# A recurrent attention layer and a split-precision FFN on one core: x loaded in both layouts, shifts on GpSimd, branch bodies exchanged, a new order on every engine

## The chip, the cores and the metric

One core of a Trainium2 chip. The metric is device time of one execution in microseconds. PE is TensorE, DVE is VectorE, ACT is ScalarE, POOL is GpSimd, SP is the engine that issues DMAs here.

## What is computed

x has 8 sequences of 1024 tokens of 128 values. The layer is a gated linear attention with 16 heads of 8 values, then a layer norm, then a gated FFN with ternary weights times scales (here multiplied by 8), then a layer norm:

```python
def step(state, inp):
    qt, kt, vt, gt = inp
    state = state * gt[..., None] + vt[..., None] * kt[..., None, :]
    out_t = jnp.einsum('bhij,bhj->bhi', state, qt)
    return (state, out_t)
...
out = (out - mu) * jax.lax.rsqrt(var + EPS) * gamma + beta
out = out * jax.nn.silu(x @ Wg)
return out @ Wout
...
h = jax.nn.silu(_tlin(x, w1_w, w1_s)) * _tlin(x, w2_w, w2_s)
h = jax.nn.gelu(_tlin(h, h1_w, h1_s), approximate=False)
h = jax.nn.gelu(_tlin(h, h2_w, h2_s), approximate=False)
return _tlin(h, w3_w, w3_s)
...
x = _layernorm(x + attention(x))
x = _layernorm(x + ffn(x))
```

Here q, k, v are x times Wq, Wk, Wv, the gate g is sigmoid(x @ Wf + bf), and the FFN is 128 to 512, 512 to 512 twice, 512 to 128.

## The kernel before

The tokens are cut into 16 blocks of 512 (two to a sequence), and block n passes through five parts on five engines. All engines run hand-ordered lists: a loop over steps s, and in each step calls for block s, s-1, s-2 and so on, so that parts of several blocks lie side by side. There is no scheduler at run time; an instruction waits on semaphores named at its start, and everything behind it on its engine waits too. The text says "step" for one turn of this loop, and the step's length is the time per block.

**Front.** transpose_x (L633) turns the four 128x128 pieces of x_in into `front`, one PSUM bank; ACT copies it to xT. From xT come k, q, the forget gate f and the output gate, one product each into the same bank `front`, each waiting until ACT has emptied it (`freed`), and v into `ps_v`. k and q go out to a buffer in HBM (`send`) and come back (`fetch`) spread over 128 partitions as KJ and QJ, 8 slices of 512, in halves of 1 MB.

**Attention on DVE.** kv (L439) multiplies v by K, two slices at a time, scan (L449) runs the recurrence for one slice, qs (L460) multiplies by Q, two slices at a time, and add (L466) folds the halves. sum_transposed on PE adds the rest while transposing, into `back`. This bank also serves norm_o, the transposed o, the product with Wout, the transposed x1, and the FFN's last product.

**Norms.** There are three per block, "o", "1" and "2". DVE takes statistics (L470) and aggregates them to mean and variance (L474) in `mv`; POOL adds eps and raises to -0.5 (rstd_of, L223 and L225); DVE multiplies -mean by rstd (shift_of, L491); ACT applies both to four chunks (L302). rstd and shift have one buffer each, so rstd_of of the next block waits for norm_done.

```python
e.tensor_tensor(rstd[k][:], mv[k][:, :, 1], eps4[:], ALU.add).then_inc(ve_done[k], 1)
e.wait_ge(ve_done[k], n + 1)
e.tensor_tensor(rstd[k][:], rstd[k][:], mhalf4[:], ALU.pow).then_inc(rstd_done[k], 1)
```

**FFN.** Values are split into a high part (ACT, a copy rounded to fp32r: x1hi, h1hi, h2hi) and a low part (POOL subtracts, L216, 512 columns each; x1lo on DVE). PE multiplies both by the weights: up_hi, up_lo (L695, L706), mid_open, mid_hi, mid_lo for two layers (L711, L737), last_begin and last_rest (L741). Silu and gelu are on ACT (L331, L344), hmul on DVE (L511), which multiplies the two halves of the gated layer.

**Low parts of the weights.** At the start the weights are split too (split_weights on ACT, wlo on POOL); their low parts are summed, counted, and the count set as a flag. PE reads the flag (value_load, then a branch) once, before step 3. If there are low parts, a body with extra products runs; if not, as here, the Else body:

```python
with e.If(n_low != 0):
    for s in range(FIRST_UP, NB + 4):
        step(s, True)
with e.Else():
    for s in range(FIRST_UP, NB + 4):
        step(s, False)
```

Of the kernel before, what the change touches and what calls it, by code (L numbers as in the profile page):

```python
# [3 lines left out]
def build_program(nc, x_d, wproj_d, wffn_d, w3_d, w3s_d, cols_d, ident_d, out_d):  # L4
# [8 lines left out]
    B, S, D = x_d.shape  # L13
# [11 lines left out]
    assert D == P and PER_SEQ == 2 and NB % 2 == 0 and NH == 4  # L25
# [6 lines left out]
    with ctx:  # L32
# [3 lines left out]
        def sem(name):  # L36
# [16 lines left out]
        mhalf4 = sb("mhalf4", [P, NC_])  # L53
        low_sum = sb("low_sum", [P, 4])
# [5 lines left out]
        xT = sb("xT", [P, T])  # L60
# [18 lines left out]
            for name, shape in (("stats", (NC_, 6)), ("mv", (NC_, 2)), ("rstd", (NC_,)), ("shift", (NC_,))))  # L79
# [13 lines left out]
        def landed(n):  # L93
# [3 lines left out]
        q_sent, k_sent, stored = ([sem(f"{k}{p}") for p in range(2)] for k in ("q_sent", "k_sent", "stored"))  # L97
        K_landed, Q_landed = (
            [[sem(f"{k}{half}_{p}") for p in range(2)] for half in range(2)] for k in ("K_landed", "Q_landed"))
        xT_made, q_made, k_made, v_made, f_made, gate_made = (  # L100
            sem(f"{k}_made") for k in ("xT", "q", "k", "v", "f", "gate"))
# [4 lines left out]
        xT_copied, q_copied, k_copied = (sem(f"{k}_copied") for k in ("xT", "q", "k"))  # L106
# [9 lines left out]
        stats_done, mv_done, ve_done, rstd_done, shift_done, norm_done = (  # L116
            {k: sem(f"{name}_{k}_done") for k in "o12"} for name in ("stats", "mv", "ve", "rstd", "shift", "norm"))
# [25 lines left out]
        def _(e):  # L143
# [30 lines left out]
            e.dma_start(ident[:], ident_d).then_inc(consts_landed, 16)  # L174
            load_x(0)
            e.dma_start(wproj[:].rearrange("p c d -> p (c d)"), wproj_d).then_inc(consts_landed, 16)
            e.dma_start(cols[:], cols_d).then_inc(consts_landed, 16)
            load_x(1)
# [5 lines left out]
            for s in range(NB + 6):  # L184
                n = s - 2
                if live(n):
                    fetch(n, 1, 0)
                    send(n, 0)
                    fetch(n, 1, 1)
                    fetch(n, 0, 0)  # L190
# [3 lines left out]
                n = s - 2  # L194
                if live(n):
                    fetch(n, 0, 1)
# [4 lines left out]
                if live(n):  # L201
                    if n > 1:
                        load_x(n)
# [7 lines left out]
        def _(e):  # L211
# [15 lines left out]
            e.wait_ge(consts_set, 5)  # L227
            for s in range(NB + 3):
                if s == 0:
                    for k, (raw, cs) in enumerate(staged):  # L230
                        e.wait_ge(whi_done, k + 1)
                        for a in range(cs.start, cs.stop, T):
                            e.tensor_tensor(wlo[:, a:a + T], raw[:, a - cs.start:a - cs.start + T], whi[:, a:a + T].bitcast(f32),
                                            ALU.subtract).then_inc(wlo_done, 1)
                    e.wait_ge(w3_landed, 32)
                    e.tensor_tensor(w3[:], w3[:], w3_scale[:].unsqueeze(1).broadcast_to([P, NH, D]), ALU.mult).then_inc(w3_scaled, 1)
                n = s - 2
                if live(n):
                    lo(2, n, 0)
                n = s - 1  # L240
                if live(n):
                    rstd_of(n, "1")
                n = s - 2
                if live(n):
                    lo(2, n, 1)
                    lo(2, n, 2)
                    lo(2, n, 3)
                n = s - 3
# [3 lines left out]
                if live(n):  # L252
                    lo(1, n, 0)
                    lo(1, n, 1)
                n = s
                if live(n):
                    rstd_of(n, "o")
                n = s - 1
                if live(n):
                    lo(1, n, 2)  # L260
                    lo(1, n, 3)

        @block.scalar
        def _(e):
            def copy_xT(n):
                e.wait_ge(xT_made, n + 1)
                if n:
                    e.wait_ge(gate_made, n)
                e.activation(xT[:], front[:], ACT.Copy).then_inc(xT_copied, 1)

# [28 lines left out]
            def normalise(n, k, dst, src):  # L299
                e.wait_ge(shift_done[k], n + 1)  # L300
                for c in range(NC_):
                    last = e.activation(dst[:, chunk(c)], src[:, chunk(c)], ACT.Identity,  # L302
                                        bias=shift[k][:, c:c + 1], scale=rstd[k][:, c:c + 1])
# [56 lines left out]
            e.wait_ge(consts_set, 5)  # L360
            for s in range(NB + 5):
                n = s - 4
                if live(n):
                    hi(1, n, 2)
                n = s - 1
                if live(n):
                    copy_k(n)
                n = s - 4
                if live(n):
                    hi(1, n, 3)  # L370
                n = s - 3
                if live(n):
                    norm_o(n)
                n = s - 1
                if live(n):
                    copy_q(n)
                    if n == 0:
                        split_weights()
                n = s - 3
                if live(n):  # L380
                    affine(n)
                n = s - 4
                if live(n):
                    gelu(1, n, 0)
                    hi(2, n, 0)
                    gelu(1, n, 1)
                    gelu(1, n, 2)
                    hi(2, n, 1)
                    gelu(1, n, 3)
                    hi(2, n, 2)  # L390
                    hi(2, n, 3)
                n = s - 3
                if live(n):
                    norm_1(n)
                    x1_hi(n)
                n = s - 4
                if live(n):
                    gelu(2, n, 0)
                n = s - 1
                if live(n):  # L400
                    tanh(n)
                    if n == 1:
                        sum_low_parts()
                n = s - 4
                if live(n):
                    gelu(2, n, 1)
                    gelu(2, n, 2)
                    gelu(2, n, 3)
                n = s - 3
                if live(n):  # L410
                    silu(n, 0)
                    silu(n, 1)
                n = s - 1
                if live(n):
                    silu_gate(n)
                    g_of_tanh(n)
# [4 lines left out]
                if live(n):  # L421
                    hi(1, n, 0)
# [4 lines left out]
                if live(n):  # L427
                    copy_xT(n)
# [482 lines left out]
```

## Time and profile before

| | us |
|---|---|
| median of 3 runs | 584.1 (582.96 to 585.02) |
| the profiled execution | 584.93 |
| its span, first to last instruction | 582.5 |
| busy: PE, DVE | 520.5, 497.1 |
| busy: ACT, POOL | 395.1, 241.1 |
| mean granted TensorE clock | 0.955 |

A page of the profile lists for each engine how long it was busy; the 40 slices show that DVE and PE are over nine tenths busy from about the fifth slice to the 35th, and that the ends are looser. The rows below are from several views: groups by line, the timeline in order of time, waits (who waited for whom), the chain of work that ended last, and busy time in windows. Ends of PE's products are modelled, so in a busy stretch the distance between starts is the better measure.

### The profile page before, as it was taken

The page shows a single profiled execution, that of the slowest core. Times are in us where ns is not written, and L with a number is a line of the kernel's source. Part 1 is how long each engine was busy: PE and PEld are TensorE (multiplying, and loading weights), DVE is VectorE, ACT ScalarE, POOL GpSimd, SP SyncE. Part 2 cuts the span into 40 slices and gives each one's busy share as a digit, 9 for nine tenths or more (in the row PEclk, how much of TensorE's full clock was granted, in tenths as well). Part 3 has the DMA queues.
Part 4 walks back from the last instruction along what each step waited for, and adds up shares of the span by engine and source line. Part 5 has one row for each costly group of instructions (what it writes and reads, how often), then busy time and mean ns, then how long its engine had stood idle before and what let it go on. Part 6 is the DMA issues. An engine that isn't in the chain of part 4 may idle for free.

```text
span 582.5 us, 7709 instructions
## 1 busy us (share of the span) xinstructions
PE 520.5 (89%) x2536; PEld 391.6 (67%) x2536; DVE 497.1 (85%) x871; ACT 395.1 (68%) x685; POOL 241.1 (41%) x239
## 2 busy tenths in 40 slices
PE   4546289999999999999999999999999999888994
PEld 1114157868787777778786878777777778666863
DVE  0397599999999999999999999999999999894311
ACT  2552157777777777777787777777777778676753
POOL 0900045152534445453616253544545362535460
PEclk9667689999999999999999999999999999899998
DMA  7899909476684929392948668593929297000001
GB/s 287 204 247 238 230 5 236 107 181 162 154 208 115 248 71 251 78 257 68 254 109 204 157 166 196 137 224 86 257 73 266 58 252 170 0 20 0 19 0 37
DMA packets 32056, 87.82 MB, mean 151 GB/s; under 512 B 2320, under 2 KB 18960, under 8 KB 23568
## 3 DMA queue, kind: packets, MB, share of 16 engines
q1 hardware_dynamic: 32016, 87.31, 60.7%
q8 instruction: 22, 0.36, 0.3%
q14 instruction: 18, 0.15, 0.1%
HBM read 74.72 MB, written 12.58 MB: 150 GB/s over the span
## 4 chain that ended last, share of the span: by engine, by line
DVE 59%; PE 19%; issue 8%; ACT 5%; POOL 4%; DMA 3%; SPq 0%; POOLq 0%; ACTq 0%
DVE KJ L449 15%; DVE QJ L460 12%; PE F L737 7%; DVE QJ L466 6%; DVE h L511 6%; DVE stats L470 4%; ACT o_norm L302 3%; DVE KJ L439 3%; DVE shift_o L491 3%; PE back L678 3%; POOL rstd_o L225 3%; DVE stats_o L470 2%; DMA KJ<-qk_bounce 2%; PE back L625 2%; PE F L711 2%
## 5 line engine op out<-in xcount | busy, mean ns | idle before, releaser
L216 POOL TENSOR_TENSOR h1lo<-h,h1hi 128x512 fp32r<-128x512 f32 x64 | 89.8, 1416 | 186.5 <-ACT h1hi L337 186.5
L216 POOL TENSOR_TENSOR h2lo<-h,h2hi 128x512 fp32r<-128x512 f32 x64 | 81.2, 1290 | 73.3 <-ACT h2hi L337 73.3
L344 ACT ACTIVATE h<-F,cols 128x512 f32<-128x512 f32 x128 | 86.4, 686 | 17.7 <-PE F L737 17.3
L439 DVE TENSOR_TENSOR KJ<-ps_v,KJ 128x1024 f32<-128x1024 f32 x64 | 77.0, 1205 | 18.6 <-DMA KJ<-qk_bounce 18.6
L711 PE MATMUL F<-h1hi,whi 128*128 128x512 f32 x256 | 80.4, 448 | 0.9 <-DVE h L511 0.7
L711 PE MATMUL F<-h2hi,whi 128*128 128x512 f32 x256 | 78.0, 438 | 0.9 <-ACT h L344 0.9
L449 DVE TENSOR_TENSOR_SCAN KJ<-g,carry,KJ 128x512 f32<-128x512 f32 x64 | 78.7, 1262 | 0.0
L460 DVE TENSOR_TENSOR QJ<-QJ,KJ 128x1024 f32<-128x1024 f32 x64 | 76.0, 1210 | 0.0
L449 DVE TENSOR_TENSOR_SCAN KJ<-g,KJ 128x512 f32<-128x512 f32 x64 | 74.7, 1201 | 0.0
L737 PE MATMUL F<-h1lo,whi 128*128 128x512 f32 x256 | 68.8, 412 | 0.0
L741 PEld LDWEIGHTS back<-w,h 128*128 128x128 f32 x512 | 61.9, 191 | 3.3 <-DVE x1lo L507 0.3
L711 PEld LDWEIGHTS F<-h2hi,whi 128*128 128x128 f32 x256 | 47.9, 188 | 23.8 <-issue 7.9
L737 PE MATMUL F<-h2lo,whi 128*128 128x512 f32 x256 | 63.6, 400 | 0.0
L711 PEld LDWEIGHTS F<-h1hi,whi 128*128 128x128 f32 x256 | 45.7, 188 | 25.6 <-issue 13.6
L741 PE MATMUL back<-w,h 128*128 128x128 f32 x512 | 62.5, 275 | 0.1
L331 ACT ACTIVATE h<-F,cols 128x512 f32<-128x512 f32 x64 | 44.0, 688 | 27.0 <-PE F L706 26.7
L737 PEld LDWEIGHTS F<-h2lo,whi 128*128 128x128 f32 x256 | 46.9, 188 | 10.3
L737 PEld LDWEIGHTS F<-h1lo,whi 128*128 128x128 f32 x256 | 47.0, 193 | 9.2
L511 DVE SCALAR_TENSOR_TENSOR h<-F,cols,h 128x512 f32<-128x512 f32 x64 | 45.2, 748 | 6.2 <-ACT h L331 6.2
L706 PE MATMUL F<-x1lo,whi 128*128 128x512 f32 x128 | 48.6, 460 | 0.0
L695 PE MATMUL F<-x1hi,whi 128*128 128x512 f32 x128 | 42.6, 414 | 2.4 <-DVE h L511 1.7
L337 ACT ACTIVATE h1hi<-h 128x512 fp32r<-128x512 f32 x64 | 39.8, 624 | 2.8 <-DVE h L511 2.8
(77 smaller groups left out, 816.6 us busy)
## 6 DMA issues: line engine op xcount, KB each, us to landing
KJ<-qk_bounce SPq DMA_DIRECT2D x32, 1024.0 KB, 12.6
QJ<-qk_bounce SPq DMA_DIRECT2D x32, 1024.0 KB, 8.3
qk_bounce<-qk SPq DMA_DIRECT2D x32, 256.0 KB, 7.3
x_in<-in_x SPq DMA_DIRECT2D x16, 256.0 KB, 8.9
out<-res SPq DMA_DIRECT2D x16, 256.0 KB, 7.7
h<-in_wffn SPq DMA_DIRECT2D x2, 1024.0 KB, 8.3
res<-in_wffn SPq DMA_DIRECT2D x2, 256.0 KB, 4.5
wproj<-in_wproj SPq DMA_DIRECT2D x1, 384.0 KB, 3.5
```

What stands on the lines that cost most here:

```text
L216: e.tensor_tensor(h_lo[layer][:, t, :], h[:, t, :], h_hi[layer][:, t, :].bitcast(f32), ALU.subtract).then_inc(lo_done[layer], 1)
L331: e.activation(h[:, t, :], F[2 * (t % 2)][:], ACT.Silu, scale=S1[t]).then_inc(silu_done, 1)
L344: e.activation(dst[:, t, :], F[t][:], ACT.Gelu, scale=scale[t]).then_inc(gelu_done[layer], 1)
L439: e.tensor_tensor(K, vb, K, ALU.mult).then_inc(kv_done, 1)
L449: e.tensor_tensor_scan(K, g[:], K, init, ALU.mult, ALU.add).then_inc(scan_done, 1)
L460: e.tensor_tensor(Q, Q, KJ[n % 2][:, 2 * p:2 * p + 2, :], ALU.mult).then_inc(qs_done, 1)
L511: e.scalar_tensor_tensor(h[:, t, :], F[2 * (t % 2) + 1][:], S2[t], h[:, t, :], ALU.mult, ALU.mult).then_inc(hmul_done, 1)
L695: e.matmul(out, whi[:, cs], x1hi[:], start=True, stop=False)
L706: last = e.matmul(out, whi[:, cs], x1lo[:], start=False, stop=True)
L711: e.matmul(F[t][:], whi[:, cs], h_hi[layer][:, k, :], start=k == 0, stop=False)
L737: last = e.matmul(F[t][:], whi[:, cs], h_lo[layer][:, k, :], start=False, stop=k == NH - 1)
L741: return e.matmul(back[:, chunk(c)], h3[:, k, chunk(c)], w3[:, k, :], start=k == 0, stop=k == NH - 1)
```

## The change

- The host's array of x is also given transposed, as 16 blocks of 128x512, and loaded as xT, in two buffers. transpose_x and the copy of xT are gone. x_in is loaded as before, and is now first needed by residual_1.
- The shifts move from DVE to POOL: POOL multiplies the mean by -1 (`minus4`) and later by rstd. rstd and shift have two buffers, so rstd_of waits for norm_done of two blocks back. DVE waits for mv_read before it overwrites mv.
- The flag is read earlier, in the middle of step 2, and the body that runs is now the If body (n_low == 0), the other is Else.
- All five lists stand in another order; a step's first call is another one, so the block indices in the code shift too. On SP, K and Q of a block are fetched in one run of four, behind both sends.

```diff
-            def transpose_x(n):
-                e.wait_ge(x_landed[n % XB], 16 * (n // XB + 1))
-                freed((gate_done, n - 1), (tanh_done, n - 1), (q_copied, n - 1), (k_copied, n - 1), (xT_copied, n - 1))
-                transpose4(front, x_in[n % XB]).then_inc(xT_made, 1)
...
             def project_k(n):
-                e.wait_ge(xT_copied, n + 1)
-                freed((xT_copied, n), (gate_done, n - 1), (tanh_done, n - 1), (q_copied, n - 1), (k_copied, n - 1))
-                e.matmul(front[:], WK, xT[:], start=True, stop=True).then_inc(k_made, 1)
+                e.wait_ge(xT_landed[n % 2], landed(n))
+                freed((gate_done, n - 1), (tanh_done, n - 1), (q_copied, n - 1), (k_copied, n - 1))
+                e.matmul(front[:], WK, xT[n % 2][:], start=True, stop=True).then_inc(k_made, 1)
...
+            def load_xT(n):
+                if n >= 2:
+                    e.wait_ge(gate_made, n - 1)
+                e.dma_start(xT[n % 2][:], xT_d[n]).then_inc(xT_landed[n % 2], 16)
...
             def rstd_of(n, k):
+                r, sh = rstd[k][:, n % 2, :], shift[k][:, n % 2, :]
                 e.wait_ge(mv_done[k], n + 1)
-                if n:
-                    e.wait_ge(norm_done[k], n)
-                e.tensor_tensor(rstd[k][:], mv[k][:, :, 1], eps4[:], ALU.add).then_inc(ve_done[k], 1)
+                if n >= 2:
+
+                    e.wait_ge(norm_done[k], n - 1)
+                e.tensor_tensor(r, mv[k][:, :, 1], eps4[:], ALU.add).then_inc(ve_done[k], 1)
+                e.tensor_tensor(sh, mv[k][:, :, 0], minus4[:], ALU.mult).then_inc(mv_read[k], 1)
                 e.wait_ge(ve_done[k], n + 1)
-                e.tensor_tensor(rstd[k][:], rstd[k][:], mhalf4[:], ALU.pow).then_inc(rstd_done[k], 1)
+                e.tensor_tensor(r, r, mhalf4[:], ALU.pow).then_inc(rstd_done[k], 1)
+                e.wait_ge(rstd_done[k], n + 1)
+                e.tensor_tensor(sh, sh, r, ALU.mult).then_inc(shift_done[k], 1)
...
-            FIRST_UP = 3
+            FIRST_UP = 2
             for s in range(FIRST_UP):
                 step(s, False)
+            step(FIRST_UP, False, second=False)
             e.wait_ge(w3_scaled, 1)
             e.wait_ge(flag_set, 1)
             n_low = e.value_load(flag[0:1, 0:1], min_val=0, max_val=P * len(staged))
-            with e.If(n_low != 0):
-                for s in range(FIRST_UP, NB + 4):
+            with e.If(n_low == 0):
+                step(FIRST_UP, False, first=False)
+                for s in range(FIRST_UP + 1, NB + 4):
+                    step(s, False)
+            with e.Else():
+                step(FIRST_UP, True, first=False)
+                for s in range(FIRST_UP + 1, NB + 4):
                     step(s, True)
-            with e.Else():
-                for s in range(FIRST_UP, NB + 4):
-                    step(s, False)
```

PE around its branch, before. The left name is written, the right ones are read; `front<-ident,x_in` is transpose_x, `back<-ident,o_norm` is transpose_y, `back<-wproj,y` the product with Wout, and L866 the branch. The body behind it starts with v:

```order
L665 MATMUL back<-ident,QJ 128x128 x16
L760 MATMUL F<-ones_col,low_any 1x1 x4
L636 MATMUL front<-xT,wproj 128x512
L641 MATMUL front<-xT,wproj 128x512
L625 MATMUL back<-ident,o_norm 128x128 x4
L678 MATMUL back<-wproj,y 128x128 x4
L865 TENSOR_LOAD flag
L865 ISA x2
L866 COMPARE_AND_BRANCH
L657 MATMUL ps_v<-xT,wproj 128x512
```

The same place on PE now:

```order
L685 MATMUL back<-ident,QJ 128x128 x16
L671 MATMUL front<-xT,wproj 128x512
L780 MATMUL F<-ones_col,low_any 1x1 x4
L885 TENSOR_LOAD flag
L885 ISA x2
L886 COMPARE_AND_BRANCH
L650 MATMUL back<-ident,o_norm 128x128 x4
L656 MATMUL front<-xT,wproj 128x512
L698 MATMUL back<-wproj,y 128x128 x4
L677 MATMUL ps_v<-xT,wproj 128x512
```

The branch moved ahead of transpose_y and of the product with Wout of block 0.

POOL in the middle of the program, before. One h2lo of a block stands ahead of norm "1", the other three behind it:

```order
L216 TENSOR_TENSOR h2lo<-h,h2hi 128x512
L223 TENSOR_TENSOR rstd<-mv,eps 128x4
L225 TENSOR_TENSOR rstd<-rstd,mhalf 128x4
L216 TENSOR_TENSOR h2lo<-h,h2hi 128x512 x3
L223 TENSOR_TENSOR rstd<-mv,eps 128x4
L225 TENSOR_TENSOR rstd<-rstd,mhalf 128x4
L216 TENSOR_TENSOR h1lo<-h,h1hi 128x512 x2
```

The same place on POOL now:

```order
L225 TENSOR_TENSOR h2lo<-h,h2hi 128x512 x4
L234 TENSOR_TENSOR rstd<-mv,eps 128x4
L235 TENSOR_TENSOR shift<-mv,minus 128x4
L237 TENSOR_TENSOR rstd<-rstd,mhalf 128x4
L239 TENSOR_TENSOR shift<-shift,rstd 128x4
L225 TENSOR_TENSOR h1lo<-h,h1hi 128x512 x4
```

Norm "1" now stands behind all four h2lo, with four small instructions in place of two.

DVE from the statistics of norm "1" on, before (an odd block):

```order
L470 BN_STATS stats<-x_in 128x6 x4
L474 BN_AGGR mv<-stats 128x2 x4
L449 SCALAR_TENSOR_TENSOR KJ<-g,carry,KJ 128x512 x2
L491 SCALAR_TENSOR_TENSOR shift<-mv,rstd 128x4
L449 SCALAR_TENSOR_TENSOR KJ<-g,carry,KJ 128x512
L470 BN_STATS stats<-res 128x6 x4
L474 BN_AGGR mv<-stats 128x2 x4
L449 SCALAR_TENSOR_TENSOR KJ<-g,carry,KJ 128x512 x2
L460 TENSOR_TENSOR QJ<-QJ,KJ 128x1024
```

The same place on DVE now:

```order
L494 BN_STATS stats<-x_in 128x6 x4
L500 BN_AGGR mv<-stats 128x2 x4
L473 SCALAR_TENSOR_TENSOR KJ<-g,carry,KJ 128x512 x2
L484 TENSOR_TENSOR QJ<-QJ,KJ 128x1024 x3
L530 TENSOR_TENSOR x1lo<-back,x1hi 128x512
L473 SCALAR_TENSOR_TENSOR KJ<-g,carry,KJ 128x512
```

The shift is gone, and two scans (not five) stand between these statistics and the first product with Q.

## Rows read from the trace of the kernel before

**Rows 1.** The page: busy us, share of the span, number of instructions.

```profile
PE 520.5 (89%) x2536; PEld 391.6 (67%) x2536; DVE 497.1 (85%) x871; ACT 395.1 (68%) x685; POOL 241.1 (41%) x239
```

**Rows 2.** Windows of two steps: length, each engine's busy us, clock, DMA share, GB/s.

```profile
200.94:232.24 31.30, 31.03 (x158) 23.80 (x158) 30.77 (x55) 23.75 (x42) 14.13 (x14) 1.00 0.66 161
232.24:263.78 31.54, 31.26 (x162) 24.23 (x161) 31.01 (x56) 24.04 (x44) 13.93 (x14) 1.00 0.69 172
```

**Rows 3.** Timeline of DVE: start and length of a block's first product.

```profile
44.72 1.22 DVE L439 TENSOR_TENSOR KJ<-ps_v,KJ 128x1024 f32<-128x1024 f32 x1
...
82.16 1.22 DVE L439 TENSOR_TENSOR KJ<-ps_v,KJ 128x1024 f32<-128x1024 f32 x1
...
491.11 1.22 DVE L439 TENSOR_TENSOR KJ<-ps_v,KJ 128x1024 f32<-128x1024 f32 x1
```

**Rows 4.** Groups by line: busy us, mean ns of one, idle before and its releaser.

```profile
L491 DVE SCALAR_TENSOR_TENSOR shift_o<-mv_o,rstd_o 128x4 f32<-128x4 f32 x16 | 18.8, 1173 | 4.4 <-POOL rstd_o L225 4.4
L225 POOL TENSOR_TENSOR rstd_o<-rstd_o,mhalf 128x4 f32<-128x4 f32 x16 | 16.1, 1006 | 1.3
L625 PE MATMUL front<-ident,x_in 128*128 128x128 f32 x64 | 11.1, 302 | 10.7 <-DMA cols<-in_cols 5.6 <-ACT gate L297 5.2
L491 DVE SCALAR_TENSOR_TENSOR shift<-mv,rstd 128x4 f32<-128x4 f32 x32 | 9.9, 310 | 16.9 <-POOL rstd L225 16.9
L223 POOL TENSOR_TENSOR rstd_o<-mv_o,eps 128x4 f32<-128x4 f32 x16 | 3.2, 198 | 36.7 <-DVE mv_o L474 36.7
```

**Rows 5.** The chain of waits: start, length, engine and line, count of merged instructions.

```profile
97.44 0.86 PE front L646 x2
98.29 2.81 PE F L711 x12
101.11 0.44 PE back L625 x4
...
548.80 2.90 PE back L741 x26
```

**Rows 6.** Timelines of DVE and POOL where both read SBUF.

```profile
110.09 3.44 DVE L466 TENSOR_TENSOR QJ<-QJ 128x1024 f32<-128x1024 f32 x2
...
111.00 1.45 POOL L216 TENSOR_TENSOR h1lo<-h,h1hi 128x512 fp32r<-128x512 f32 x1 [10.05 <-ACT h1hi L337]
...
254.85 2.52 POOL L216 TENSOR_TENSOR h2lo<-h,h2hi 128x512 fp32r<-128x512 f32 x2
...
255.78 0.36 DVE L491 SCALAR_TENSOR_TENSOR shift<-mv,rstd 128x4 f32<-128x4 f32 x1
```

**Rows 7.** The chain at the end of the program: the last block's three shifts.

```profile
528.98 1.25 DVE shift_o L491
...
538.83 1.26 DVE shift L491
...
577.77 0.17 DVE shift L491
```

**Rows 8.** Timeline of ACT: the table load ahead of a block's first gelu.

```profile
249.30 1.28 ACT L344 ACT_TABLE_LOAD   x1
```

**Rows 9.** The page's DMA issues (median us to landing), and the chain's first send.

```profile
KJ<-qk_bounce SPq DMA_DIRECT2D x32, 1024.0 KB, 12.6
...
11.54 3.92 DMA qk_bounce<-qk
```

**Rows 10.** The first long step: waits, the window behind the branch, timelines of ACT and DVE.

```profile
PE ps_v L657 <- issue: 7.6, 1, 7.6
...
PE back L625 <- issue: 3.1, 1, 3.1
...
55.70:66.00 10.30, 2.67 (x9) 2.16 (x10) 9.23 (x17) 1.65 (x4) 1.21 (x2) 0.51 1.05 246
...
62.13 1.65 ACT L302 ACTIVATE x<-x_in,shift,rstd 128x128 f32<-128x128 f32 x4 [7.59 <-DVE shift L491]
...
73.38 0.69 DVE L507 TENSOR_TENSOR x1lo<-back,x1hi 128x512 fp32r<-128x512 f32 x1 [6.62 <-ACT x1hi L324]
```

More of the change, by code:

```diff
@@ L201, in _ @@
                 if live(n):
[L202 to L203 removed]
+                    load_x(n)
+                n = s - 1
+                if live(n):
+                    send(n, 0)
+                n = s
+                if live(n):
+                    if n > 1:
+                        load_xT(n)
+                n = s - 1
+                if live(n):
+                    fetch(n, 1, 0)
+                    fetch(n, 1, 1)
+                    fetch(n, 0, 0)
+                    fetch(n, 0, 1)
             for p in range(2):
@@ new lines, in rstd_of, with weights_lo @@
+                e.wait_ge(rstd_done[k], n + 1)
+                e.tensor_tensor(sh, sh, r, ALU.mult).then_inc(shift_done[k], 1)
+            def weights_lo(pair):
+                for a in (2 * pair * T, (2 * pair + 1) * T):
+                    k = sum(a >= cs.stop for _, cs in staged)
+                    raw, cs = staged[k]
+                    e.wait_ge(whi_done, k + 1)
+                    e.tensor_tensor(wlo[:, a:a + T], raw[:, a - cs.start:a - cs.start + T], whi[:, a:a + T].bitcast(f32),
+                                    ALU.subtract).then_inc(wlo_done, 1)
@@ L359, in _ @@
             e.wait_ge(consts_landed, 48)
-            e.wait_ge(consts_set, 5)
+            e.wait_ge(consts_set, 6)
             for s in range(NB + 5):
[L362 to L416, printed above, removed]
                 n = s - 5
@@ L612, in _ @@
                     kv(n, 0)
+                n = s - 2
+                if live(n):
+                    hmul(n, 2)
+                n = s - 1
+                if n == 0:
+                    find_low_parts()
+                n = s - 2
+                if live(n):
+                    hmul(n, 3)
+                n = s
+                if live(n):
+                    kv(n, 1)
+                n = s - 1
+                if live(n):
+                    stats_o(n)
+                n = s
+                if live(n):
+                    scan(n, 0)
+                n = s - 1
+                if n == 0:
+                    set_flag()
+                n = s - 3
+                if live(n):
+                    stats_2(n)
+                n = s
+                if live(n):
+                    scan(n, 1)
+                    scan(n, 2)
+                    kv(n, 2)
+                    kv(n, 3)
+                n = s - 1
+                if live(n):
+                    gated_y(n)
+                n = s
+                if live(n):
+                    scan(n, 3)
+                n = s - 1
+                if live(n):
+                    residual_1(n)
+                n = s
+                if live(n):
+                    scan(n, 4)
+                n = s - 1
+                if live(n):
+                    stats_1(n)
+                n = s
+                if live(n):
+                    scan(n, 5)
+                    scan(n, 6)
+                    qs(n, 0)
+                    qs(n, 1)
+                    qs(n, 2)
+                n = s - 1
+                if live(n):
+                    x1_lo(n)
+                n = s
+                if live(n):
+                    scan(n, 7)
         @block.tensor
```

406 lines of the change are left out of this document (199 added, 207 removed).

## The prediction

> **What bounds the kernel now.** I read the page first, then the windows of two whole blocks, then the chain of waits, then the start. The page gives DVE 497.1 and PE 520.5 of a span of 582.5 us [rows 1]. In the middle, where all blocks overlap, both are full: of 31.30 and 31.54 us a block, PE is busy 31.03 and 31.26, DVE 30.77 and 31.01 [rows 2]. ACT has 24 and POOL 14 us, so they bound only where something waits in line behind them. The first product of block 1 on DVE (k times v, L439) starts at 44.72, that of block 2 at 82.16 and that of block 15 at 491.11 [rows 3]: a step in the middle takes (491.11 - 82.16) / 13 = 31.46 us, but the step before it took 37.44. The rest is 44.7 us of start and 91.4 of end. So there are three places to look at: the step, the long first step, and the ends.
>
> **The step, PE.** Per block the change removes four transposes of x. The row of these has 64 with 11.1 us busy, 0.69 a block; four transposes of this size take 0.44 in the chain [rows 4, 5]. The projections, the FFN products and the rest stay. An independent sum from rates of the chain: 80 products of 512 columns at 2.81 / 12 = 0.234 us are 18.7; five projections at 0.86 are 4.3; 56 instructions of 128 columns (32 of w3, 8 of Wout, 16 summing transposes) at 2.90 / 26 = 0.112 are 6.3; two groups of four transposes at 0.44 are 0.9 [rows 5]. That makes 30.2 us after the change with no wait at all, 30.6 before. From the windows it is 31.15 (mean of the two) less 0.44 = 30.7, which has today's small waits in it.
>
> **The step, DVE.** The change takes the three shifts off DVE: 18.8 us in 16 of shift_o and 9.9 in 32 of the others, 28.7 / 16 = 1.8 us a block [rows 4]. They are 512 numbers each; shift_o costs 1.17 us because it is late, not because it works. The clearest row is the shift at 255.78: it lasts 0.36 us and ends at 256.14, just where the first of POOL's two subtractions from 254.85 ends (2.52 / 2 = 1.26 each); alone, the last shift of the program takes 0.17 [rows 6, 7]. DVE then has 30.9 - 1.8 = 29.1 us of work a step. The other DVE work is only put in another order. ACT loses the copy of xT; with 24 of 31 us busy that hides, and if it did not it would be another gain.
>
> So PE becomes the bound. I take **30.7 us a step**: bounds are 30.2 (PE without waits) and 31.5 (no gain). One wait I expect to stay inside the 30.7: on ACT the group for block n-3 now runs norm_o, the table load of 1.28 us with gelu 0, gelu 1, then affine and the first h2hi, whereas before affine stood ahead of the table load [rows 8]. The h2hi opens layer 2 on PE. Adding these up after shift_o I find PE waiting some 0.4 to 0.6 us for h2hi; the bare 30.2 with that gives 30.6 to 30.8, the same number again. From the first product of block 2 to that of block 15 are 13 steps, and block 15's own attention is one more: 14 x (30.7 - 31.46) = **-10.6 us**.
>
> **POOL.** It gets six more instructions of 128x4 a block. The nearest row is the addition of eps, 0.20 us; so 6 x 0.2 = 1.2 us on an engine with 14 of 31 busy [rows 2, 4]. On the path of a norm, before: add 0.20, pow 1.01, shift on DVE 1.17 or 0.31. After: add 0.20, times -1 0.20, pow 1.01, product 0.20. For "o" that is 1.61 against 2.38, a gain; for "1" about the same. Both ends: nothing, or one wait behind a DVE instruction for each.
>
> **SP.** Each block also loads 256 KB of xT, beside 4 MB of K and Q copies. DMA is busy 0.66 to 0.69 of a step at 161 to 172 GB/s [rows 2]: 256 KB more are 5% more traffic, 1 us in 10 spare. The order of SP moves too: K and Q of a block are fetched in one run behind both sends, so K can land later before its use than now. ACT copies q at about 24 us into PE's step, the K product is due some 11 us after that; a fetch of K has a median of 12.6 us to land with others queued [rows 9]. I cost it at nothing, covered by the queue that is now empty ahead of it; uncovered, it is 1 to 2 us a step. The new waits (mv_read on DVE, gate_made before load_xT) are for work a step or more old.
>
> **The long first step.** DVE sits 6.6 us idle before x1lo of block 0, since x1hi comes late, since PE stands 7.6 us and then 3.1 us more for "issue", that is, for nothing that a semaphore shows [rows 10]. The 7.6 begin right behind the instruction that reads the flag and branches. The path taken is the Else body, which stands behind the whole body with the low products; while PE stands, DMA is full (1.05) [rows 10]. In the changed kernel the condition is turned, so the body that runs is the next code, and the branch comes earlier, right behind the count and ahead of transpose_y. I take the whole idle time as gone: **-6.6 us**. Bounds: 0, if the wait is the reading of the flag or a full DMA, and -6.6. Nothing is late next there: norm_1 of block 0 ends at 63.8, so with a transpose and a copy x1hi could be there near 65.2, before DVE is ready for it at 66.8 [rows 10].
> The Trainium skill (Runtime: NRT & Kernel Launch, section "Instruction fetch mechanics") says that code is fetched ahead only in sequence and that a taken branch to code outside the window stalls on a fetch; by that rule the stall goes wholly. No run here shows yet what a branch that falls through costs.
>
> **The start.** K of block 0 leaves for the bounce buffer at 11.54 and is there at 15.46; then its fetch is sent [rows 9]. Without x's transposes and their copy, k is there some 1.4 us earlier. Against it, 0.5 MB of x and xT are in the queue before K and Q, at 165 / 0.67 = 246 GB/s for a full DMA [rows 2] about 2 us. I take 0, between -1.4 and +1.5.
>
> **The end.** In the last block the shifts stand in the chain with 1.25, 1.26 and 0.17 [rows 7]; in their place come 0.2 + 0.27 each. That is -2.68 + 1.41 = **-1.3 us**. Both ends of this are near: the products of these sizes have rows.
>
> **Sum.** The profiled execution took 584.93 us for its span of 582.5, 0.8 above the median of 584.1. 584.93 - 10.6 - 6.6 + 0 - 1.3 = **566.4 us**. All good ends together: 14 x (30.2 - 31.46) = -17.6, -6.6, -1.4, -1.3: 558.0. A difference under 0.3% could not be told from none.
>
> **Rivals.**
> - *The PE stall only moves.* It is then a wait of 7.6 us ahead of transpose_y. For it speaks that DMA is just as full there, and that a second stall of 3.1 us came with no branch. Against it, that both lie within 15 us of the only branch and nowhere else. y of block 0 comes some 5 us late: 566.4 + 5 = 571.4. Chance 18%.
> - *The step stays at 31.46.* Two engines that both run at 98% wait for each other's results, and the new order has new ones, as h2hi. Then only start and end gain: 584.93 - 6.6 - 1.3 = 577.0. Chance 18%.
> - *Slower: the norm on POOL is locked out.* In the new order rstd_1 stands behind all four h2lo and not behind one, and three Q products of DVE (two SBUF operands) follow two scans behind stats_1. What such a pair does is to be seen at 110.09: POOL's subtraction began during the first addition on DVE and took 1.45 us, and DVE's two additions took 3.44 in place of 2.36 [rows 6]. So each waits out the other's instruction. By my addition the last of the four small instructions ends within 0.2 us of the first Q product. If three of them wait 1.2 us each, x1hi is 3.6 us late, of which 1.0 is spare: 30.7 + 2.6 = 33.3 a step, 14 x 1.84 - 7.9 = +17.9, 602.8 us. It decides from 32.0 us a step, 1.3 us of lateness. One alone that waits gives 31.9 and no change, 583. Chance 12%: 3 for no change, 9 for slower. Against it speaks that POOL did get in between the two additions there, and so need wait for one only.
> The Trainium skill (SBUF — State Buffer, section "Who interferes with whom") states it as an exclusive lock between a GpSimd read and a DVE instruction with two SBUF inputs; the trace agrees, by the 3.44 us. By this rule alone, moving work onto GpSimd costs when it meets Q products, and gives the 602.8 us.
>
> **How the numbers follow.** Forecast 52%, the others 18, 18 and 12. The first three are faster: 88%; same 3%, slower 9%. The range goes from 558, all good ends, to 578, just over the second rival; outside are the third and a bit of the tails.
>
> **What would show it.** Right: first products of blocks 2 to 15 at a distance of 30.7; PE busy over 99% of a step and DVE near 29.1 with small waits for x1hi, y and hmul; POOL's small products at 0.2; no PE wait over 2 us behind the branch, and no 6.6 before x1lo; block 2's first product near 75.5 us. Wrong: a step of 31.4; a wait of POOL's small rows over 1 us; DVE waiting for KJ; PE standing some 7 us at about 52 us. If both DVE and PE are under 97% in a step, orders and not work bound it.

## The result and the profile after

The changed kernel takes 569.41 us (median of 4 runs, 569.22 to 570.64), the kernel before 584.46 beside it; the ratio is 0.9751 (95% interval 0.9727 to 0.9774). So it is faster, inside the range of 558 to 578, and 3.0 us above the forecast of 566.4. The profiled execution took 569.22 us with a span of 567.4.

The page after, busy us of each engine, as [rows 1]:

```profile
PE 507.2 (89%) x2472; PEld 382.8 (67%) x2472; DVE 485.1 (85%) x824; ACT 378.2 (67%) x669; POOL 248.0 (44%) x335
```

Windows of two steps after (length, then busy us by engine, clock, DMA share, GB/s), as [rows 2]:

```profile
199.60:230.70 31.10, 30.78 (x156) 23.70 (x155) 30.14 (x53) 22.87 (x41) 14.54 (x21) 1.00 0.74 179
230.70:261.77 31.07, 30.76 (x156) 23.67 (x155) 30.60 (x52) 22.87 (x41) 14.50 (x21) 1.00 0.72 175
```

The first product of blocks 1, 2 and 15 on DVE after, as [rows 3]:

```profile
47.82 1.23 DVE L463 TENSOR_TENSOR KJ<-ps_v,KJ 128x1024 f32<-128x1024 f32 x1 [1.93 <-DMA KJ<-qk_bounce]
...
76.07 1.21 DVE L463 TENSOR_TENSOR KJ<-ps_v,KJ 128x1024 f32<-128x1024 f32 x1
...
479.37 1.21 DVE L463 TENSOR_TENSOR KJ<-ps_v,KJ 128x1024 f32<-128x1024 f32 x1
```

These cut both spans into the same four pieces. The lists have another order now, so the border between the first two pieces does not fall at quite the same work:

| piece | before | after | difference | forecast |
|---|---|---|---|---|
| start, to block 1's first product | 44.72 | 47.82 | +3.1 | 0 |
| the long first step | 37.44 | 28.25 | -9.2 | -6.6 |
| 13 steps | 408.95 | 403.30 | -5.7 | -9.9 |
| the rest | 91.39 | 88.03 | -3.4 | -2.1 |

The sum is -15.1; what lies outside the span adds -0.6. Up to block 2's first product (the first two pieces together) it is 76.07 against 82.16, -6.1 us, where -6.6 was forecast. A step takes 403.30 / 13 = 31.02 us where I forecast 30.7. DVE should have had 29.1 us of work in it and has 30.1 to 30.6. The groups by line of the changed kernel show what the extra microsecond is:

```profile
L477 DVE COPY carry<-KJ 128x8 f32<-128x8 f32 x16 | 17.0, 1065 | 0.0
...
L235 POOL TENSOR_TENSOR shift_o<-mv_o,minus 128x4 f32<-128x4 f32 x16 | 3.2, 201 | 0.0
L239 POOL TENSOR_TENSOR shift_o<-shift_o,rstd_o 128x4 f32<-128x4 f32 x16 | 3.2, 199 | 1.3
```

and the same copy in the kernel before, groups by line:

```profile
L453 DVE COPY carry<-KJ 128x8 f32<-128x8 f32 x16 | 2.6, 161 | 0.0
```

The copy of the carry, 8 numbers in each partition, takes 1065 ns on average where it took 161: 13 of the 16 take 1.21 to 1.24 us, the other three 0.17, 0.43 and 0.67. The timelines of POOL and DVE in one step of the changed kernel say why:

```profile
198.36 2.53 POOL L225 TENSOR_TENSOR h1lo<-h,h1hi 128x512 fp32r<-128x512 f32 x2 [11.13 <-ACT h1hi L354]
...
198.47 1.21 DVE L477 COPY carry<-KJ 128x8 f32<-128x8 f32 x1
```

The first of POOL's two subtractions runs from 198.36 to about 199.6, and the copy, which began 0.11 us behind it, ends at 199.68. It is the picture of the shift at 255.78 in [rows 6]: the wait for POOL was not removed from DVE but handed from one small instruction to another. Being small is not all there is to it. In the same step four aggregations run beside POOL's h2lo in 0.38 us, as everywhere:

```profile
211.74 5.04 POOL L225 TENSOR_TENSOR h2lo<-h,h2hi 128x512 fp32r<-128x512 f32 x4 [3.32 <-ACT h2hi L354]
...
216.00 0.38 DVE L500 BATCH_NORM_AGGREGATE mv<-stats 128x2 f32<-128x6 f32 x4
```

The small ones that the traces show held up are the shift and the copy. The chain of waits of the changed kernel (start, length, what), one turn of it:

```profile
198.47 1.21 DVE carry L477
199.68 1.13 DVE KJ L463
200.81 0.67 DVE h L534
...
201.50 0.64 ACT h1hi L354
...
202.21 1.02 POOL h1lo L225
...
203.45 1.29 POOL h1lo L225
...
205.05 0.96 POOL rstd_o L237
...
206.38 1.51 ACT o_norm L319 x4
...
207.91 1.28 ACT L361
...
209.20 0.64 ACT h L361
...
210.36 0.75 ACT back L330
211.11 0.56 ACT h2hi L354
...
211.71 0.74 PE F L731 x2
...
226.02 2.92 PE back L761 x26
...
229.56 1.21 DVE carry L477
```

The same copy stands at both ends, 31.09 us apart. So the step is a closed loop through four engines: the copy holds up a product and hmul, these ACT and POOL, these the norm "o", then come the table load (ACT L361, 1.28 us), gelu, affine and h2hi, which PE waits for, and PE's last products of the block release residual_2 and with it the next copy. Busy time alone does not show it: PE is busy 30.77 of 31.08 us, and only moving the copy (run 1) shows that PE was not what set the step.

### The profile page after: what moved, and what is told of

Same layout as the page of the kernel before. It is cut to its first block, busy times and chain, and to the rows that moved or that the text cites. A ratio compares the mean times of both kernels' runs of the same rounds, so it can differ in the third digit from the quotient of the medians.

```text
span 567.4 us, 7658 instructions
## 1 busy us (share of the span) xinstructions
PE 507.2 (89%) x2472; PEld 382.8 (67%) x2472; DVE 485.1 (85%) x824; ACT 378.2 (67%) x669; POOL 248.0 (44%) x335
## 4 chain that ended last, share of the span: by engine, by line
PE 50%; ACT 16%; DVE 11%; POOL 11%; DMA 6%; issue 5%; SPq 0%; ACTq 0%; POOLq 0%; DVEq 0%
PE F L731 11%; PE F L757 10%; PE back L761 10%; POOL h1lo L225 6%; DMA qk_bounce<-qk 4%; ACT o_norm L319 4%; PE F L715 3%; DVE KJ L463 3%; PE F L726 3%; ACT L361 3%; DVE carry L477 3%; PE back L698 2%; POOL rstd_o L237 2%; PE front L666 2%; PE front L661 2%
## 5 line engine op out<-in xcount | busy, mean ns | idle before, releaser
L225 POOL TENSOR_TENSOR h1lo<-h,h1hi 128x512 fp32r<-128x512 f32 x64 | 82.9, 1316 | 192.1 <-ACT h1hi L354 192.1
L361 ACT ACTIVATE h<-F,cols 128x512 f32<-128x512 f32 x128 | 81.0, 685 | 7.0 <-PE F L757 6.8
L731 PE MATMUL F<-h2hi,whi 128*128 128x512 f32 x256 | 76.4, 431 | 4.0 <-ACT h2hi L354 2.4
L731 PE MATMUL F<-h1hi,whi 128*128 128x512 f32 x256 | 73.1, 427 | 4.1 <-DVE h L534 4.0
L757 PE MATMUL F<-h2lo,whi 128*128 128x512 f32 x256 | 70.9, 419 | 0.0
L757 PE MATMUL F<-h1lo,whi 128*128 128x512 f32 x256 | 70.0, 416 | 0.0
L348 ACT ACTIVATE h<-F,cols 128x512 f32<-128x512 f32 x64 | 44.0, 689 | 19.6 <-PE F L726 19.4
L298 ACT ACTIVATE qk<-front 128x512 f32<-128x512 f32 x16 | 9.6, 599 | 66.1 <-PE front L661 66.1
L354 ACT ACTIVATE h1hi<-h 128x512 fp32r<-128x512 f32 x64 | 38.3, 623 | 16.1 <-DVE h L534 16.1
```

The lines of the kernel that those rows point to most:

```text
L225: e.tensor_tensor(h_lo[layer][:, t, :], h[:, t, :], h_hi[layer][:, t, :].bitcast(f32), ALU.subtract).then_inc(lo_done[layer], 1)
L348: e.activation(h[:, t, :], F[2 * (t % 2)][:], ACT.Silu, scale=S1[t]).then_inc(silu_done, 1)
L354: e.activation(h_hi[layer][:, t, :], h[:, t, :], ACT.Copy).then_inc(hi_done[layer], 1)
L361: e.activation(dst[:, t, :], F[t][:], ACT.Gelu, scale=scale[t]).then_inc(gelu_done[layer], 1)
L731: e.matmul(F[t][:], whi[:, cs], h_hi[layer][:, k, :], start=k == 0, stop=False)
L757: last = e.matmul(F[t][:], whi[:, cs], h_lo[layer][:, k, :], start=False, stop=k == NH - 1)
```

## The experiments

Theory A: the loop sets the step, and the copy's wait for POOL is part of it. Theory B: PE's work sets it. Later runs take the parts of the change apart. All times are medians of 4 runs (10 for the kernel with x transposed alone); since runs were on several chips, the ratio to the kernel before on the same chip is the measure.

| run | us | ratio to before | 95% interval |
|---|---|---|---|
| the changed kernel | 569.41 | 0.9751 | 0.9727 to 0.9774 |
| 1 copy early | 555.76 | 0.9516 | 0.9468 to 0.9564 |
| 2 table early | 566.65 | 0.9701 | 0.9649 to 0.9752 |
| 3 both | 555.60 | 0.9517 | 0.9468 to 0.9566 |
| 4 bodies back | 576.51 | 0.9873 | 0.9809 to 0.9937 |
| 5 before, bodies exchanged | 578.68 | 0.9905 | 0.9879 to 0.993 |
| 6 before, x transposed | 583.84 | 0.9998 | 0.998 to 1.0016 |
| 7 before, shifts on POOL | 568.50 | 0.9723 | 0.9699 to 0.9748 |
| 8 four edits | 558.52 | 0.956 | 0.9537 to 0.9584 |
| 9 before, three parts | 562.45 | 0.9654 | 0.9624 to 0.9683 |
| 10 K first | 557.09 | 0.9565 | 0.9534 to 0.9596 |
| 11 x late | 555.25 | 0.9536 | 0.9509 to 0.9563 |
| 12 q of block 1 first | 556.08 | 0.9551 | 0.9523 to 0.958 |

### 1. The copy of the carry early

```diff
                     add(n, 0)
+                    save_carry(n)
                     qs(n, 3)
...
-                n = s - 1
-                if live(n):
-                    save_carry(n)
```

> The changed kernel with the copy of the carry (DVE, 8 columns) moved from behind residual_2 to behind the first addition, where POOL does nothing. Theory A: a loop through several engines sets the step of 31.08 us, and in it the copy's 1.21 us, of which 1.05 are a wait for POOL's h1lo. Then the copy takes 0.16, the step falls to between 30.2 and 30.7 and the kernel to about 562 us (558 to 566). Theory B: PE's own work sets the step, as it is busy 30.77 of 31.08; then the copy gets short but the step stays at 31.0 and the time at 569.

Measured: 555.76 us, below even what A expected. The copy in the groups by line, and two windows of a step, from one block's first product to the next one's:

```profile
L477 DVE COPY carry<-KJ 128x8 f32<-128x8 f32 x16 | 2.6, 164 | 0.0
```

```profile
196.54:226.58 30.04, 30.04 (x156) 23.84 (x155) 29.16 (x53) 22.83 (x42) 14.58 (x21) 1.00 0.76 183
226.58:256.62 30.04, 30.04 (x156) 23.82 (x155) 29.64 (x52) 22.80 (x42) 14.57 (x21) 1.00 0.76 184
```

PE is busy 30.04 of 30.04 us, and the chain there is PE alone. The step fell by 0.98 us (31.02 to 30.04), and the copy by 0.90. B falls: in the changed kernel PE's work did not set the step; in run 1 it does. And the sum of rates in the prediction, 30.2 us for PE with no wait, is met to 0.2.

### 2 and 3. The table load early, alone and with the copy

```diff
+                n = s - 3
+                if live(n):
+                    e.activation(early[:], half_bf[:], ACT.Gelu)
                 n = s - 2
                 if live(n):
                     norm_o(n)
```

> The changed kernel with one gelu of one column put ahead of norm_o on ACT, so that the table load of 1.28 us runs in the 2 us in which ACT waits for shift_o. Nothing else moved. Theory A (a loop through norm_o, table load, gelu, affine and h2hi): y and h2hi come up to 1.28 us earlier, the step falls to 30.2 to 30.6, the kernel to 557 to 564 us. Theory B (PE's work): 569, no change; PE's waits for h2hi shrink but appear elsewhere.

> Both of these edits. Theory A: PE is then the bound with 30.2 us of work; step 30.2 to 30.5, kernel 556 to 561 us, and less gain than the sum of the two. Theory B: 569.

The load moved where it was meant to go, as ACT's timeline of run 2 shows; ACT's wait before o_norm is 0.46 us where it was 1.98:

```profile
203.77 1.28 ACT L404 ACT_TABLE_LOAD   x1
205.07 0.20 ACT L404 ACTIVATE early<-half_bf 128x1 f32<-128x1 f32 x1
205.73 1.51 ACT L320 ACTIVATE o_norm<-back,shift_o,rstd_o 128x128 f32<-128x128 f32 x4 [0.46 <-POOL shift_o L240]
```

But the step fell only from 31.02 to 30.83 us ((477.03 - 76.25) / 13), not to 30.6 or less. A was right about the loop and wrong about its size here: with the branch through the norm shortened, the chain of run 2 goes from the copy over the product and hmul straight to PE, and the copy is in that turn too:

```profile
197.82 1.21 DVE carry L481
199.03 1.13 DVE KJ L467
200.16 0.67 DVE h L538
...
200.96 1.30 PE F L735 x4
...
228.64 1.20 DVE carry L481
```

There are two loops, 31.1 and 30.8 us long. They share the stretch from PE's last products and residual_2 over the copy, the product and hmul; in it the copy is what was not needed, and the table load is in the first alone. The time, 566.65 us, lies between A's 557 to 564 and B's 569. With the copy early the table load is worth nothing more (run 3, same ratio as run 1): PE is full.

### 4 and 5. The bodies of the branch

Run 4 is the changed kernel with the old order of bodies, run 5 the kernel before with the new:

```diff
-            with e.If(n_low == 0):
-                step(FIRST_UP, False, first=False)
+            with e.If(n_low != 0):
+                step(FIRST_UP, True, first=False)
...
             with e.Else():
-                step(FIRST_UP, True, first=False)
+                step(FIRST_UP, False, first=False)
```

> The changed kernel with the two bodies of the branch in the old order again: the body that runs is Else, behind the long one. If the branch to far code was the cause of PE's 7.6 us in the kernel before, the same wait of 7 to 8 us stands now behind the flag at about 53 us, transpose_y of block 0 comes 5 to 6 us late, and the kernel takes 574 to 576 us. If the flag's reading or a full DMA was the cause and only the place of the branch mattered, the time stays at 569 to 570.

> The kernel before with only the two bodies of the branch exchanged (condition turned, so the body that runs is the next code). From the run that turned them back in the changed kernel (7 us slower) the stall of 7.6 us behind the flag should go: 577 to 578 us, DVE's 6.6 us before x1lo gone. If the second stall of 3.1 us is a matter of its own, DVE still waits 1 to 3 us there: 579 to 581.

PE's timeline behind the branch in the changed kernel, where it falls through:

```profile
51.14 0.34 PE L780 MATMUL F<-ones_col,low_any 128*1 128x1 f32 x8
...
54.82 1.09 PE L650 MATMUL back<-ident,o_norm 128*128 128x128 f32 x4 [3.34 <-ACT o_norm L319]
```

in run 4, where it jumps (the 11.36 us hold the wait for o_norm as well):

```profile
61.47 1.08 PE L650 MATMUL back<-ident,o_norm 128*128 128x128 f32 x4 [11.36 <-issue]
```

and in run 5, the kernel before, where it falls through too, with 0.16 us in place of the 7.6 of [rows 10]:

```profile
56.89 2.00 PE L657 MATMUL ps_v<-xT,wproj 128*128 128x512 f32 x2 [0.16 <-issue]
```

The transposes of block 0's o come 6.65 us later in run 4, and the kernel is 7.1 us slower by the two medians, just above the 574 to 576 expected; its four times lie between 573.83 and 579.14. Run 5 starts block 2 at 75.73 on DVE and not at 82.16, so 6.4 us of the 37.44 were the jump, and its time is 5.4 us lower than the kernel before beside it. The time lies between the two expectations, but DVE waits nothing before x1lo, so the first theory holds. A full DMA alone is not the cause: from 50 to 55 us, where the changed kernel falls through, its DMA share is 1.04. The second stall of 3.1 us is gone as well, so it belonged to the jump.
The Trainium skill (Runtime: NRT & Kernel Launch, "Instruction fetch mechanics") says that code is fetched ahead in sequence and a jump outside the window waits for a fetch; the two runs agree that the jump costs, with 7.1 and 5.4 us, at a time when the core's DMA is full. That PE waits for just such a fetch is what the Trainium skill says; no row here shows it.

### 6, 7 and 9. The parts in the old order

Run 6, x loaded transposed, is the change's own edit of the projections and load_xT put into the kernel before, with x_in's first loads behind the weights. Run 7 is the change's rstd_of, minus4, mv_read and the two buffers, and on DVE:

```diff
-                    shift_of(n, "o")
...
-                    shift_of(n, "1")
...
-                    shift_of(n, "2")
```

Run 9 has both and the exchanged bodies; only the new orders are missing.

> The kernel before with only x loaded transposed: no transposes of x on PE, no copy of xT on ACT, all else in the old order. If DVE's list was the bound of the old step (31.46 us), PE's 0.44 us are worth nothing: step 31.3 to 31.5, time 582 to 585. If PE was the bound, the step falls by 0.44 and the time to 577 or 578.

> The kernel before with only the shifts moved to POOL and two buffers for rstd and shift, all else in the old order. If DVE's list was the bound, up to 1.7 us a step go until PE's 30.6 us of work stop it: step 30.7 to 31.0, time 574 to 578. If the wait for POOL's lock only moves to the next DVE instruction of this kind (the copy of the carry, right behind), the step stays near 31.2 and the time above 580.

> The kernel before with three parts of the change (x loaded transposed, shifts on POOL with two buffers, bodies exchanged) and all lists in the old order, so that only the new orders are missing. In the old order the copy of the carry takes 0.16 us (run with the shifts alone: step 30.52, all of it PE's). Theory: the new orders cost what the copy of the carry waits, and the parts gain the rest: PE's 30.1 us of work set the step, 5 us go at the branch, so 559 to 563 us, 6 to 10 below the changed kernel. Rival: the old order has waits of its own once PE is so full, step 30.5 to 31, and the time is 565 to 570.

x transposed alone is worth nothing (ratio 0.9998): the step is 31.47, as before, though PE has four transposes less: PE did not set the old step. It also brings the later start: block 1's first product is at 47.15 in run 6 and at 47.38 in run 9, both with SP's old order of fetches, against 44.72 before. The shifts alone are worth 15.6 us, as much as the whole change. Groups by line and windows of run 7:

```profile
L458 DVE COPY carry<-KJ 128x8 f32<-128x8 f32 x16 | 2.5, 159 | 0.0
```

```profile
205.35:235.53 30.18, 30.18 (x158) 23.88 (x157) 29.07 (x52) 23.44 (x42) 15.32 (x21) 1.00 0.72 175
235.53:266.32 30.79, 30.79 (x161) 24.47 (x161) 29.73 (x52) 24.11 (x43) 14.94 (x21) 1.00 0.70 171
```

In the old order POOL's h1lo 2 and 3 stand behind rstd_o and begin 0.44 us after the copy has ended (241.14 against 240.54 + 0.16), so no small DVE instruction meets them any more; PE is busy all of both windows, mean 30.48, with the transposes of x still in it (30.6 was the sum in the prediction). This is below the 574 to 578 that I expected: I took 30.7 to 31.0 for the step, and it is (479.36 - 82.59) / 13 = 30.52. Against the lower end of 574 the step makes 2.3 us of the difference; more came after block 15's first product, where run 7 takes 87.44 us and the kernel before 91.39.
Run 9 then gives 562.45, inside its expectation. Its step, from the first products at 78.07 and 473.43, is 30.41 us and not PE's 30.04; the chain goes through DVE (scan, Q products, additions, residual_2) and `back`. So both theories for it hold in part: the old order is 0.4 us a step above PE's 30.04, the new order with the copy where it is 1.0. The new orders (with the new place of the branch) cost 0.0097 of the ratio, 5.7 us; with the copy early they would have gained 1.4% over run 9, 8 us.

### 8, 10, 11 and 12. The start

Run 8 has four edits: those of runs 1, 2, 10 and 11. Runs 10 to 12 each stand on run 1.

```diff
                 n = s - 1
                 if live(n):
+                    fetch(n, 1, 0)
+                    fetch(n, 1, 1)
                     send(n, 0)
...
-                    fetch(n, 1, 0)
-                    fetch(n, 1, 1)
                     fetch(n, 0, 0)
```

```diff
                 n = s
-                if live(n):
-                    load_x(n)
...
                     fetch(n, 0, 1)
+                n = s
+                if live(n):
+                    load_x(n)
```

```diff
                 n = s
+                if n == 1:
+                    project_q(n)
                 if live(n):
                     project_v(n)
...
-                if live(n):
+                if live(n) and n != 1:
                     project_q(n)
```

> The changed kernel with four edits: the copy of the carry early, the table load early, on SP the fetches of K ahead of the send of q, and the load of x behind the fetches. The first two alone gave 555.6 us with a step of 30.1, which is PE's work. The other two concern the start: block 1's first product waited 1.9 us for K, and block 0's K left 1.8 us later than in the kernel before. If DMA order sets the start, it gains 2 to 4 us: 552 to 554. If the start is set by the total of bytes, 555 to 556.

> The changed kernel with the copy of the carry early (555.8 us) and, on SP, the fetches of K ahead of the send of q. If block 1's first product waits for K because its fetch stands behind q's send (39.77 us), it starts 2 us earlier: 553 to 554.5. If the queue's bytes decide, 555 to 556, and this was not what made the kernel with all four edits slower (558.5).

> The changed kernel with the copy of the carry early (555.8 us) and the load of x behind the four fetches. Block 0's K leaves for the bounce buffer with 256 KB less ahead of it, about 1 us: 554 to 555.5. If this edit is what made the kernel with all four slower, 557 to 559.

> The changed kernel with the copy of the carry early (555.8 us) and, for block 1 only, the product for q ahead of that for v, which waits on DVE's kv of block 0. Then K of block 1 is fetched at about 26 us and not at 39.8, and block 1's first product no longer waits for it (1.9 us): 553 to 555. If DMA's bytes decide there, 555 to 556.

What they were after is in the timeline of SP of the changed kernel: k leaves at 9.97, 1.6 us earlier than before, and its fetch follows 7.3 us later, where it was 3.9:

```profile
9.97 0.34 SPq L160 DMA_DIRECT2D qk_bounce<-qk  x1
...
17.30 1.26 SPq L174 DMA_DIRECT2D KJ<-qk_bounce  x2
```

Block 1's first product on DVE in runs 10, 11 and 12:

```profile
49.15 1.22 DVE L463 TENSOR_TENSOR KJ<-ps_v,KJ 128x1024 f32<-128x1024 f32 x1 [2.10 <-DMA KJ<-qk_bounce]
```

```profile
46.30 1.22 DVE L463 TENSOR_TENSOR KJ<-ps_v,KJ 128x1024 f32<-128x1024 f32 x1 [1.75 <-DMA KJ<-qk_bounce]
```

```profile
47.02 1.22 DVE L463 TENSOR_TENSOR KJ<-ps_v,KJ 128x1024 f32<-128x1024 f32 x1 [0.97 <-DMA KJ<-qk_bounce]
```

Run 1 has it at 48.25. But the five kernels whose start differs in nothing but the place of one copy (the changed one and runs 1 to 4) have it at 47.82, 48.25, 46.16, 46.53 and 46.64. So the 46.30 and 47.02 of runs 11 and 12 show no gain, and K's fetch first, with 49.15 here and 48.97 in run 8, is 0.7 to 0.9 us later than the latest of the five.
Run 12 also shows that the expectation had the wrong cause. The send that had waited for ACT leaves at 24.74 and no longer at 38.27 (run 1), yet the fetch of K is issued at 39.32 after 40.24. The waits of SP in run 12 (20 to 42 us; total, times, longest) say what it stood for, K's own copy to HBM (sent at 21.91) and no engine:

```profile
SPq L174 <- DMA qk_bounce<-qk: 14.0, 2, 13.8
```

None of it is clear in the times: the intervals of 1, 11 and 12 overlap. Runs 8 and 10 came out above both of their expectations (558.52 and 557.09 us against at most 556). That K first is what made run 8 slower than run 3 fits both, and is not shown beyond that. The DMA share is 0.93 or more in every 5 us from 20 to 50 us of the changed kernel and of run 1; with run 12's wait this speaks for the bytes in the queue as what sets this start, which no run tests by itself.

Run 1's version and run 11's (555.25 us) beat both kernels, by 27 to 28 us against the kernel before and some 13 against the changed one; I can't tell the two apart.

## Why the prediction was right, and where not

The forecast was 3.0 us off, and that is in part luck. The steps gave 4.2 us less than forecast and the start 3.1 less; the long first step gave 2.6 more, the end 1.3 more, and what lies outside the span 0.6. The mechanism of the step was wrong: PE's work was to set it, and a loop through four engines did. The sign named for that, both engines under 97%, did not show it, since PE was busy for 99% of the step all the same.

**The long first step** (-6.6): right, and it was the jump. Runs 4 and 5 give 7.1 and 5.4 us in the time, and run 5 has 6.4 in the piece itself. The other 2.8 of the piece's -9.2 were not in my sum for it. In the kernel before with the bodies exchanged the piece is 31.11 us. There DVE stands 2.56 us for PE before block 0's statistics at 48.47; in the new order block 1's second kv product comes ahead of them and no such wait is left. In run 9, with the old orders, the piece is 30.69. Most of the 2.8 only makes up for the late start: block 2's first product is at 75.73 in run 5 and at 76.07 in the changed kernel.

**The step, DVE** ("DVE then has 30.9 - 1.8 = 29.1 us"; "the other DVE work is only put in another order"): this is the step of the prediction that failed. The first half is right, run 1 has 29.2 to 29.6. The second half is wrong: the new order set the carry's copy beside POOL's first h1lo, and order alone cost 0.9 us of DVE time. I had read in [rows 6] that a small DVE instruction sits out POOL's whole subtraction, and had priced that only for POOL's own small instructions against the Q products. I had not gone through DVE's new list for other small instructions that run while POOL does, and the copy of the carry is one, of 161 ns.
The Trainium skill (SBUF — State Buffer, "Who interferes with whom") names copies among the instructions that can contend with GpSimd for the shared pair, if their operands meet its conditions; the trace agrees, with 1065 ns against 164.

**The step, PE**: the floor of 30.2 us without waits holds (30.04 in run 1), and 30.6 with x's transposes too (30.48 in run 7). "From the windows less 0.44 = 30.7" took over DVE's waits as if they were PE's work: busy times of PE in a step that is bound elsewhere are stretched. The step term was mis-sized by this and the copy: -9.9 forecast for 13 steps, -5.7 measured; without the copy's wait, as in run 1, it is 13 x (30.04 - 31.46) = -18.5.

**ACT's order** (table load between norm_o and affine): the wait is real and on the chain, but was worth 0.2 us a step by itself (run 2).

**POOL**: 0.20 us for each small instruction, as taken. The rival of the locked norm did not come. In the step shown above, POOL's last small instruction of norm "1" begins at 218.12 and the first Q product at 218.51. The margin was 0.2 us, and the mechanism struck elsewhere.

**SP and the start** (0, between -1.4 and +1.5): wrong, +3.1. I had said that K might land later and costed it at nothing in the step, which holds (no wait for KJ after block 1). At the start the cover is not there: the fetch of the first K is issued 1.8 us later, with 256 KB more in the queue, and block 1's first product waits 1.93 us for K. Runs 6 and 9 have 47.15 and 47.38 with SP's old order, so loading x in both layouts is enough for the late start, and by run 12 the send of q is not the only thing that held K's fetch. Five kernels with the same start scatter from 46.16 to 48.25, so the +3.1 itself is good to some 1 to 2 us. Up to block 2's first product the start and the jump together are -6.1, and the forecast's 0 for all but the jump is near (76.07 against 75.73).

**The end** (-2.1 with the 14th step): -3.4. Run 7 has 87.44 us for this piece and runs 5 and 6 have 91.48 and 91.37, so it goes with the shifts on POOL. One term was not in the sum. In the kernel before, eight products took 3.25 us there and not the usual 1.87:

```profile
500.04 3.25 PE F L737 x8
```

Their granted clock was down: 0.70 on average from 500 to 505 us, so in part at 1.2 and in part at 2.4 GHz, after PE had been busy 2.99 of the 5 us before, with 2.01 us of waiting for o_norm. Runs 5 and 6 have the same (2.92 and 3.32 us). With the shifts on POOL, in run 7 and 9, these products take 1.86 and 1.87 us at a clock of 1.00, and the changed kernel's clock is 1.00 there too. That is 1.4 us of the 3.4; the 14th step is 0.4, and the shifts' 1.3 was not measured by itself.

**That the parts add up**: 5.4 (bodies) and 15.6 (shifts) and 0 (x) would be 21; together in the old order they are 0.0346 of the ratio, 20.2 us. Taking x's transposes away as well (run 9 against run 7) gives 0.1 us a step, 30.41 against 30.52, where PE has 0.44 less to do. The new orders then took 5.7 back.

## What to carry to other kernels

If a small VectorE instruction shows a microsecond and its siblings a tenth, look at what GpSimd runs at its start; moving that instruction away only helps if no other one comes to stand there, so after each reordering go through the list for every small VectorE copy or two-input instruction that falls beside a GpSimd one. When two engines are at 98%, look for a loop in the chain, the same instruction at a distance of just one step: here a wait that was in both loops was worth nearly its full length per step, until PE was full, and one that was in one of them 0.2 us. Put the body of a branch that will run right behind it, and build the floor of an engine from its rates in a stretch where it never waits, not from its busy time.

## What I had not expected of the hardware

- One copy of 128x8 numbers, moved over five instructions of the same engine, is worth 13.7 us of 569 (0.9751 to 0.9516): 13 of its 16 waits were of over 1 us, and nearly all of them on the path.
- A jump over the unused body cost PE 7.6 us and then 3.1 more some instructions later, while a branch that falls through cost 0.16 us. Both stalls went with the jump.
- With PE at work without a gap for 30.04 us a step, its granted clock stays at 1.00 (2.4 GHz) in both windows of run 1; it is no lower for being busy all the time. In the kernel before it was 0.70 from 500 to 505 us, after PE had been busy for only 2.99 of 5 us.
- A send issued 13.5 us earlier (run 12) let the fetch behind it go only 0.9 us earlier: SP then stood 13.8 us for a copy of 256 KB to land, in a full queue.
